# One-core graph network kernel: degrees, `join` and key tables moved to the passes' tails, constants loaded ahead of the flag, group 0's one-hot and addition moved ahead of own one-hots

## The reference, cut to what matters

```python
for _ in range(2):                                  # passes 0 and 1
    edge_input = concat([h[src], h[dst], edge_attr])  # 128 + 128 + 32
    m_ij = relu(edge_input @ We1 + be1) @ We2 + be2
    h = h + segment_sum(m_ij, dst)
x = layernorm(x + h + bias)
deg = segment_sum(edge_weight, dst) + 1             # loops have weight 1
dinv = rsqrt(deg)
h = segment_sum((x @ W.T)[src] * dinv[src] * edge_weight * dinv[dst], dst)   # pass 2
out = layernorm(x + relu(h + bias1) + x)
```

## Time and profile before

| | |
|---|---|
| median of 3 runs | 2439.45 us (2436.54 to 2440.81) |
| the profiled execution, its time and span | 2436.7 us, 2434.5 us |
| TensorE busy, matmul | 2195.3 us (90%) |
| GpSimd busy | 1700.0 us (70%) |
| VectorE busy | 1396.8 us (57%) |
| ScalarE busy | 895.7 us (37%) |
| granted TensorE clock, mean | 0.939 of full speed |
| passes 0 and 1, first to last gather | 49.0 to 956.0 us, 1005.5 to 1916.4 us |

### The profile page before, as it was taken

One profiled execution on the slowest core, in us unless ns is written; L12 is line 12 of the kernel. 1 busy time (PEld: TensorE's weight loads), 2 busy tenths in 40 slices (PEclk: granted clock), 3 DMA queues, 4 the chain that ended last, 5 costly groups with the idle time before them and its releaser, 6 DMA issues.

```text
span 2434.5 us, 49886 instructions
## 1 busy us (share of the span) xinstructions
PE 2195.3 (90%) x14876; PEld 1723.8 (71%) x15066; DVE 1396.8 (57%) x3830; ACT 895.7 (37%) x1461; POOL 1700.0 (70%) x1772
## 2 busy tenths in 40 slices
PE   2899999999999998899999999999998679999996
PEld 2677676666666666676666666666666579999996
DVE  2765555655555542465555555555553467777875
ACT  2443334444443432243434444433434332322322
POOL 3677777777777775277777777777777377677763
PEclk8899999999999995699999999999998689999998
DMA  5333333333333332333333333333333211111111
GB/s 143 88 105 100 102 102 101 102 102 102 102 101 101 102 97 86 100 90 101 102 101 102 102 98 100 102 100 100 102 101 101 64 48 51 49 49 49 48 47 50
DMA packets 156158, 218.67 MB, mean 90 GB/s; under 512 B 73955, under 2 KB 107609, under 8 KB 155950
## 3 DMA queue, kind: packets, MB, share of 16 engines
q0 software_dynamic: 56272, 115.27, 18.4%
q1 hardware_dynamic: 92638, 98.41, 14.1%
q10 hardware_dynamic: 7168, 4.09, 0.7%
HBM read 207.48 MB, written 10.12 MB: 89 GB/s over the span
## 4 chain that ended last, share of the span: by engine, by line
POOL 45%; issue 29%; PE 18%; DMA 3%; DVE 3%; ACT 1%; POOLq 1%; SPq 0%; DVEq 0%; ACTq 0%
POOL gat L524 44%; PE ps L709 6%; PE ps L718 6%; PE ps L595 3%; DMA gat<-dst_row 1%; PE ps L792 1%; DMA gat<-p_dram,idx 1%; DMA gat<-z_dram,idx 1%; PE ps L788 1%; DMA cbase_dram<-cint 0%; PE ps L658 0%; PE ps L634 0%; DVE node_a L1206 0%; PE ps L618 0%; PE ps L584 0%
## 5 line engine op out<-in xcount | busy, mean ns | idle before, releaser
L524 POOL DMA_INDIRECT gat<-p_dram,idx x1422 | 1364.0, 959 | 471.4 <-issue 430.7
L658 PE MATMUL ps<-node_a,x 128*128 128x512 bf16 x2210 | 679.9, 382 | 11.0 <-issue 1.1
L1225 DVE TENSOR_TENSOR msg<-ps,gat 128x512 f32<-128x512 f32 (+1 forms) x404 | 252.8, 627 | 680.6 <-DMA gat<-p_dram,idx 592.3
L595 PE MATMUL ps<-hot,msg 128*128 128x64 f32 x3232 | 449.3, 287 | 99.7 <-ACT msg L910 86.6
L1206 DVE TENSOR_SCALAR node_a<-ps,row_id 128x512 bf16<-128x512 f16 x1200 | 486.5, 475 | 47.2 <-PE ps L641 35.3
L595 PEld LDWEIGHTS ps<-hot,msg 128*128 128x128 f32 x3232 | 408.9, 200 | 129.6 <-ACT msg L910 108.9
L658 PE MATMUL ps<-node_a,adj 128*128 128x512 bf16 x1200 | 458.6, 382 | 0.0
L584 PEld LDWEIGHTS ps<-rhs,lhs 96*128 96x128 f32 x3232 | 408.7, 199 | 53.8 <-ACT lhs L891 23.4
L584 PE MATMUL ps<-rhs,lhs 96*128 96x128 f32 x3232 | 412.6, 283 | 24.4 <-ACT lhs L891 16.5
L524 POOL DMA_INDIRECT gat<-z_dram,idx x328 | 321.9, 982 | 160.4 <-issue 100.7
L658 PEld LDWEIGHTS ps<-node_a,x 128*128 128x128 bf16 x2400 | 237.0, 102 | 243.7 <-issue 9.4
(11 more groups left out here) (154 smaller groups left out, 1787.8 us busy)
## 6 DMA issues: line engine op xcount, KB each, us to landing
dbc<-dst_row SPq DMA_DIRECT2D x202, 256.0 KB
lhs<-eaT SPq DMA_DIRECT2D x202, 128.0 KB
gat<-p_dram,idx POOLq DMA_INDIRECT x1422
rhs<-q_dram SPq DMA_DIRECT2D x202, 32.0 KB
gat<-z_dram,idx POOLq DMA_INDIRECT x328
idx<-src_g SPq DMA_DIRECT2D x243, 4.0 KB
p_dram<-node_a ACTq DMA_DIRECT2D x12, 256.0 KB
q_dram<-node_b SPq DMA_DIRECT2D x12, 256.0 KB, 3.5
```

Source lines behind the costliest of these rows:

```text
L524: return pool.indirect_dma_start(out=out_, out_offset=None, in_=table, in_offset=bass.IndirectOffsetOnAxis(ap=index, axis=0))
L595: last = nc.tensor.matmul(ps_agg(s), (msg if p < 2 else gat)[s][:, c, :], hot[s][:, c, (0 if p < 2 else 1), :], start=(c == 0), stop=(c == ...
L658: mm = nc.tensor.matmul(ps_own, p_part[k][:, t, :], shot[j % 2][:, t - t0, :, :].rearrange("p j e -> p (j e)"), start=(t == 0 and k == 0), ...
L1225: V.tensor_tensor(msg[s][:, c0:c1, :], ps_pre(s, h)[:, 0:(c1 - c0) * P].rearrange("p (c f) -> p c f", f=P), gat[s][:, c0:c1, :], ALU.add). ...
```

## The change

Five edits. (1) The loads of `be2_row`, `we2`, `w1t` and `bias1_bc` move on SyncE's queue ahead of the wait for the flag. (2) On ScalarE the one-hot of group 0 moves ahead of the second round of table casts; in pass 1 no root stands ahead of either. (3) On VectorE own part 2 moves, in step 0 of each pass, from ahead of the addition of group 0 to behind the next one-hot. (4) `chunk_keys` is cut in two, which run in steps 96 and 97 of pass 0. (5) In pass 1 the degree products follow the sums of group 94, VectorE's degree operations stand in step 95, the root in ScalarE's step 96 and `join` in step 97.

```diff
+DEG_AT = 4 * BATCHES - 2
...
             for s in range(2):
                 sp.dma_start(rhs[s][W:W + CE, :], We1[2 * P:2 * P + CE, :]).then_inc(rhs_const[s], 16)
+            sp.wait_ge(dve_const, 2)
+            sp.dma_start(be2_row[0:1, :], be2.rearrange("(a n) -> a n", a=1)).then_inc(const_in, 16)
+            sp.dma_start(we2[:, :], We2).then_inc(const_in, 16)
+            sp.dma_start(w1t[:, :], W1T).then_inc(const_in, 16)
+            sp.dma_start(bias1_bc[:, :], bias1.rearrange("(a n) -> a n", a=1).to_broadcast([P, P])
+                         ).then_inc(const_in, 16)
             sp.wait_ge(flag_ready, 1)
...
-                if p == 1:
-
+
+                def degree_products():
                     for t in range(TILES):
-                        mm = nc.tensor.matmul(ps[:, 7, t:t + 1], cw[:, t * P:(t + 1) * P], parts[:, 0:1],
+                        mm = nc.tensor.matmul(ps_deg[:, t:t + 1], cw[:, t * P:(t + 1) * P], parts[:, 0:1],
                                               start=True, stop=True)
                     mm.then_inc(deg_mm, 1)
...
                         sums(g, s)
+                        if p == 1 and type(g) is int and g == DEG_AT:
+                            degree_products()
...
                             nc.scalar.activation(m, m, ACT.Relu).then_inc(relu_done, 1)
+                            if p == 1 and type(g) is int and g == DEG_AT + 2:
+                                degree_roots()
...
                             nc.scalar.copy(p_part[0][:, t0:t0 + n, :], node_a[:, t0:t0 + n, :]).then_inc(part_cut, 1)
+                        if p == 0:
+                            act.wait_ge(rel_ready, 2)
+                        one_hots(0, 0, 1)
                         for q, (t0, n) in enumerate(QUADS):
                             n = min(n, HI - t0)
                             act.wait_ge(part_left, 2 * len(QUADS) * p + q + 1)
                             nc.scalar.copy(p_part[1][:, t0:t0 + n, :], rest[:, t0:t0 + n, :]).then_inc(part_cut, 1)
-                        act.wait_ge(rel_ready, 2)
-                        one_hots(0, 0, 1)
...
-                        if q is not None and j < 3:
+                        first = type(g) is int and g == 0
+                        if first:
+                            pass
+                        elif q is not None and j < 3:
                             own_hots(j + 1, q)
...
-                        if type(g) is int and g == 1:
-                            (chunk_keys if p == 0 else join)()
+                        if first:
+                            own_hots(j + 1, q)
+                        if p == 0 and type(g) is int and g == DEG_AT + 2:
+                            chunk_lanes()
+                        if p == 0 and type(g) is int and g == DEG_AT + 3:
+                            chunk_columns()
+                        if p == 1 and type(g) is int and g == DEG_AT + 1:
+                            degrees()
+                        if p == 1 and type(g) is int and g == DEG_AT + 3:
+                            join()
```

More of the change, by code:

```diff
@@ L195, in build @@
         ps_own = ps[:, 6, :]
+        ps_deg = ps[:, 7, 0:TILES]
         ps_ids = ps[:, 7, :].bitcast(f16)[:, 0:4 * P]
@@ L419, in _ @@
                                      node_b[:, t0:t0 + n, :]).then_inc(z_out, 16)
-                if p == 0:
-                    sp.dma_start(be2_row[0:1, :], be2.rearrange("(a n) -> a n", a=1)).then_inc(const_in, 16)
-                    sp.dma_start(we2[:, :], We2).then_inc(const_in, 16)
-                    sp.dma_start(w1t[:, :], W1T).then_inc(const_in, 16)
-                    sp.dma_start(bias1_bc[:, :], bias1.rearrange("(a n) -> a n", a=1).to_broadcast([P, P])
-                                 ).then_inc(const_in, 16)
                 with sp.If(fast == 1):
@@ L754, in _ @@
                             pe.wait_ge(ids_kept, 2)
-                        else:
-                            pe.wait_ge(dchain, 1)
                         turn_ids(0)
@@ L768, in _ @@
                 with pe.Else():
+                    if p == 1:
+                        degree_products()
                     with pe.Fori(0, NG) as g:
@@ L878, in _, with degree_roots @@
                             split_weight(k)
-                    else:
+                    def degree_roots():
                         act.wait_ge(dchain, 3)
@@ L1056, in chunk_keys, with chunk_columns @@
                 V.tensor_copy(lane_lof[:, :], lane_lo[:, :]).then_inc(chunk_ready, 1)
+            def chunk_columns():
                 dve.wait_ge(chunk_ready, 9)
@@ L1147, in _, with degrees @@
                     else:
-                        dve.wait_ge(deg_mm, 1)
-                        V.tensor_scalar_add(deg[:, :], ps[:, 7, 0:TILES], 1.0).then_inc(dchain, 1)
-                        dve.wait_ge(dchain, 1)
-                        V.tensor_single_scalar(dmask[:, :], deg[:, :], 0.0, ALU.is_gt).then_inc(dchain, 1)
-                        dve.wait_ge(dchain, 2)
-                        V.tensor_copy(dtmp[:, :], ones[:, 0:1].to_broadcast([P, TILES])).then_inc(bounds, 1)
-                        dve.wait_ge(bounds, 14)
-                        V.copy_predicated(dtmp[:, :], dmask[:, :].bitcast(mybir.dt.uint32), deg[:, :]
-                                          ).then_inc(dchain, 1)
-                        dve.wait_ge(agg_clear, 2)
+                        dve.wait_ge(agg_clear, 2)
+                def degrees():
+                    dve.wait_ge(deg_mm, 1)
+                    V.tensor_scalar_add(deg[:, :], ps_deg, 1.0).then_inc(dchain, 1)
+                    dve.wait_ge(dchain, 1)
+                    V.tensor_single_scalar(dmask[:, :], deg[:, :], 0.0, ALU.is_gt).then_inc(dchain, 1)
+                    dve.wait_ge(dchain, 2)
+                    V.tensor_copy(dtmp[:, :], ones[:, 0:1].to_broadcast([P, TILES])).then_inc(bounds, 1)
+                    dve.wait_ge(bounds, 14)
+                    V.copy_predicated(dtmp[:, :], dmask[:, :].bitcast(mybir.dt.uint32), deg[:, :]
+                                      ).then_inc(dchain, 1)
                 with dve.If(fast == 1):
@@ L1323, in _ @@
                     if p == 1:
+                        degrees()
                         join()
                     if p == 0:
-                        chunk_keys()
+                        chunk_lanes()
+                        chunk_columns()
                         V.memset(lhs[0][0:W, :], 0.0).then_inc(g_group, 1)
```

2 lines of the change are left out of this document (1 added, 1 removed).

## The result

The changed kernel took 2429.7 us in the median of 15 runs (2421.87 to 2435.12), the kernel before 2438.82 us in 15 runs on the same chip (2436.03 to 2441.07): ratio 0.9962, interval 0.9954 to 0.9971. That is 9.1 us less, inside the range of 2415 to 2431, but 7.2 us above the 2422.5 that was forecast. The profiled execution took 2429.68 us (span 2427.9). The runs of the changed kernel lie 13 us apart, those of before 5.

A forecast was written before the change was run, and what follows sets the result against it. GpSimd's back-to-back gathers were taken to set the pace inside the edge passes. Gains of 7.1 us in pass 0 and 9.7 in pass 1 sum to 16.8, giving 2422.5 us, range 2415 to 2431.

The forecast's parts named there:

- The openings: Start of both edge passes: GpSimd's wait after its first 16 gathers shrinks; group 4 starts 7.8 and 13.0 us earlier.
- group 4: Its gathers wait for group 2's addition; forecast to start at 92.3 us in pass 0 and 1046.5 in pass 1.
- TensorE's way: Openings: from the first own one-hots to group 2's addition, forecast 23.7 us in pass 0 and 21.4 in pass 1.
- the clock that rises late: TensorE's clock in pass 1's opening: 1 us added to the start of group 4.
- rival (a): Openings become TensorE's: lower clock up to 2.6 and 4 us, loads 1.5 late each; gain 8, about 2431; chance 0.12.
- The tails: Ends of both passes: key tables cost 0.7 us, `join`'s hold 3.3, degree work nothing.
- The degree products: Pass 1's tail: 8.87 us of TensorE work under 9.3 us of cover, taken at nothing.
- The constants: Four loads ahead of the flag: taken at nothing, at most 0.7 us if they delay the flag.
- the key tables: Pass 0's tail: split over steps 96 and 97, they lengthen some gathers and cost 0.7 us.
- the 5.5 taken: Openings: time for group 0's destinations load to land after issue, 5.5 us, kept at 4 to 7.

The follow-up runs named there:

- b_open: Kernel before with only group 0's one-hot ahead of ScalarE's second casts and own part 2 behind the next one-hot: 2430.78 us, ratio 0.9975.
- a_const: Kernel before with only the four constant loads moved ahead of the flag's wait: 2433.39 us, ratio 0.9987.
- c_tails: Kernel before with only key tables, degree products, degree operations, root and `join` moved into the tails: 2430.13 us, ratio 0.9971.
- the second comparison: Both kernels run again unedited on one chip: changed kernel 2436.48 us, kernel before 2443.21 us, ratio 0.9972.
- the turned order: Changed kernel with extra TensorE products, `join`'s sum at pass 1's head and the one-hot ahead of the window addition in both passes: 2402.99 us, ratio 0.9836.
- l_late_before: Kernel before with three tiny memsets ahead of each VectorE one-hot in pass 1: 2425.42 us, ratio 0.9929.
- j_late: Changed kernel with three tiny memsets ahead of each VectorE one-hot in pass 1: 2419.79 us, ratio 0.9936.
- i_early: Changed kernel with the next one-hot ahead of the window addition in pass 1: 2419.35 us, ratio 0.9933.
- f_warm: Changed kernel with matrix products nobody reads, 26 or 16 ahead of group 0's products and 8 behind, in both openings: 2424.45 us, ratio 0.9946.

## Why the prediction came out as it did

**The openings** came by the forecast's mechanism. GpSimd's waits fell from 10.26 and 11.52 to 1.83 and 0.58 us, and group 4 then set the gain, by TensorE's way. Its way to group 2's addition was 24.2 us in pass 0 (69.04 to 93.28; forecast 23.7) and 23.8 in pass 1 (1020.25 to 1044.00; forecast 21.4). For the clock that rises late I added 1 us in pass 1 and nothing in pass 0; measured against the pass's first gather, group 4 came 1.3 us later than forecast in each. The extra products gave 1.5 and 0.7 of that back: rival (a) came true in this part, and not as a whole. One more thing was not foreseen: in pass 1 the next gather starts 1.76 us late behind group 4's first one. Of this, 0.42 us are a one-hot's hold (that gather lasts 1.36, the one-hot began 0.14 us ahead of it), and then GpSimd stands idle for 1.65 us and not 0.30. The trace names no releaser. `b_open` has such a gap (1.31), and so has every kernel here that holds edits 2 and 3, while `a_const`, `c_tails` and before have none; its cause was not found.

**The tails** came as forecast. The degree products were covered, 9.31 us against 9.3. `join` cost 2.36 us in one gather, against 3.3; the 0.30 of the gather ahead of it is a one-hot's hold, as its end shows (0.82 us behind that one-hot's, see below).

**The constants** were put at nothing ahead of the flag, at most 0.7. The flag came 1.15 us later in the first comparison, and, in the means, 1.2 and 1.7 us later in the other two by the flag times above. This term was mis-sized, and the table's first row has it.

**The step that failed** stands in the first part: "So inside a pass GpSimd sets the pace, and a microsecond is saved where GpSimd stands still or is held, and nowhere else", read as if the rest of a pass kept its length. I looked for holds at the places that the change touches, `join` and the key tables, and took the 0.94 and 0.30 us as fixed elsewhere. They are not: the middle of pass 1 loses 6 to 21 us to held gathers by where VectorE's one-hot falls, and the changed kernel lost more in both comparisons (6.2 and 2.2 us more). Pass 0's middle and tail gave back 2.2 us and, in the second comparison, 5.6, where 0.7 was forecast. In the first pair most of it is in the small lengthenings of pass 0's middle, gathers of 0.96 to 1.2 us: they cost 4.4 us in sum after and 2.6 before (2.6 and 1.3 in the second pair; 0.4 with the turned order). What makes them was not studied.

**Near which rival it came.** By its number, a gain of 9.1 lies outside the forecast's own 12 to 21 and next to rival (a)'s 8, at 2431. That is a coincidence: (a) wanted 5.6 us more of TensorE and loads 1.5 us late in each pass, and the runs show 2.6 us of lateness in the openings, loads within 0.4 us of the 5.5 taken, and the rest in held gathers of mid-pass, which no rival names. The range held the time only because its upper end is made of (a)'s terms, the clock and the load.

**How much of the shortfall is which.** From pass 0's first gather to pass 1's last the change gained 5.4 us in the first pair of profiles (1866.5 to 1861.1) and 4.4 in the second (1876.0 to 1871.6). With the one-hot out of the way in pass 1 in both kernels it gained 10.5 (`l_late_before` 1861.4 to `j_late` 1851.0) or 13.1 (to `i_early`, 1848.3). So the holds explain 5 to 9 of the 11 to 12 us that this stretch lacks against the forecast of 16.8; of the rest, 2.6 are group 4's lateness in the two openings and 1.8 the late second gather of group 4 in pass 1 (1.35 of it unexplained). Each is one profile against one, and `l_late_before` ran on another chip than the other two. What stays open is why the changed kernel falls on the wrong side of a start more often: two profiles of each kernel, with 13 and 39 held gathers against 26 and 44, do not tell a property of the kernel from scatter. The pass 2 that the change does not touch was 473.5 to 482.7 us long over all these kernels; that scatter was not studied.

## What to carry to other kernels

When one engine issues back to back for hundreds of microseconds, look at the mean duration of its instruction and at the few long ones before costing anything else, and ask which engine's two-input operation starts beside them. Such an operation is best placed by time, not by what it depends on: between two starts it held no gather here. On the last chip three tiny writes in the kernel before were worth 17.8 us, and the five edits of the change 6.7. And if a first burst on TensorE is moved ahead of a wait, keep the engine busy over the wait.

## What the runs showed of the hardware

The hold has a sharp edge, and on either side of it one of the two waits. In four profiles (both of before, both of after) I took for each of the 614 gathers in the middle of pass 1 the start of the nearest one-hot.

- *One-hot first.* Every gather that lasted over 1.2 us had the one-hot at least 0.044 us ahead of its own start, and up to 0.27. Such a gather ends 0.81 to 0.83 us behind the end of the one-hot, and so lasts from 1.23 to 1.47 us. The same holds for `join`: it ends at 1888.60 and the gather beside it at 1889.42.
- *Gather first.* Every other gather had it at most 0.044 ahead, or behind, and lasted 0.94 to 0.96 us, but for two beside which it was nearly over (0.49 and 0.55 ahead, 1.01 and 0.94 us). Now the one-hot is the one that is stretched: where it starts between 0.044 us ahead of the gather and 0.024 behind, it ends 0.721 to 0.725 us behind the gather's start, and lasts up to 0.767 us in place of 0.69. That was so for 163 of the 352 one-hots. It is never held to the gather's end, and one that starts 0.03 us or more behind is not stretched at all.

The timeline of the changed kernel has a one-hot that came just too late to hold its gather:

```profile
1209.00 0.77 DVE L1086 TENSOR_TENSOR hot<-iota_row,drel 128x512 f32<-128x512 f32 x1
...
1209.05 0.94 POOL L526 DMA_INDIRECT gat<-p_dram,idx  x1 [0.30 <-issue]
```

So losing costs VectorE 0.08 us at most and GpSimd 0.5, and right at the edge the gather lasts 0.94 or 1.46 us. In pass 0 the edge lies elsewhere for some: a gather of 1.51 us had its one-hot start 0.015 us behind it (`after`, at 128.17), and why was not studied. The median distance in pass 1 was 0.00 and -0.04 us in the two profiles of before, -0.02 and -0.05 in the two of after, and +0.03 in `l_late_before`: so a few hundredths of a microsecond decide over 15 us. Between the two profiles of before, whose spans differ by 8.6 us, the held gathers differ by 12.6; that they also make the medians of the last comparison longer (before at 2443 and not 2436 us) was not tested. That the distances stay so near to zero fits VectorE's addition being released by the landing of a gather, at a fixed distance from GpSimd's issues; this was not tested either.

The Trainium skill ("SBUF — State Buffer", section "SBUF: two separate sides") says that a VectorE operation with two SBUF inputs and a GpSimd operation that reads SBUF share a port pair as an exclusive lock, and that whichever starts first holds it for its whole instruction and blocks the other. The traces agree that one of the two waits and that an operation of VectorE that is ahead keeps the gather waiting until its own end, for a one-hot of 0.69 us and for `join`'s 3.68 alike. They differ for the gather that is ahead: it keeps the one-hot waiting for 0.08 us at most, and not for its own 0.94.

While the 52 degree products of one column ran, back to back for 9.31 us, the granted clock fell: it was 1.00 from 1850 to 1858.9 us, before them, and 0.50 from 1863 to 1868.3, though TensorE was never idle. It was still 0.50 from 1872 to 1880, after them. In `f_warm` the extra products fill the stretch ahead of the own ones, and those then ran at a mean granted clock of 1.00 (71 to 79 us) where in the changed kernel the first 3.7 us of them had 0.52.
